# Lora A loaded in place by 32 register-addressed transfers instead of a gather and transposes

## What is computed

```python
# conditional layer, per sequence b
A, Bm = lora_As[itok], lora_Bs[itok]            # (32, 512, 16), (32, 16, 512)
xt = x @ W.T + b + 2 * ((x @ A) @ Bm)
# router
scores = softmax(xt @ router_w + router_b) + router_bias
gate = top 2 of the experts in the best 2 of 4 groups, weighted by their scores
# experts and shared expert
y = sum_e gate_e * ((silu(xt @ w1_e + b1_e) * (xt @ w2_e + b2_e)) @ w3_e + b3_e)
z = (silu(xt @ sw1 + sb1) * (xt @ sw2 + sb2)) @ sw3 + sb3
out = x + y + z
```

## Time and profile before

| | us |
|---|---|
| median of 3 runs (130.16 to 131.28) | 130.21 |
| the profiled execution's own time | 131.28 |
| its span, first to last instruction | 129.5 |
| PE busy in the span | 123.5 |
| DVE busy | 86.0 |
| ACT busy | 48.3 |

### The profile page before, as it was taken

One profiled execution on the slowest core, in us unless ns is written; L12 is line 12 of the kernel. 1 busy time (PEld: TensorE's weight loads), 2 busy tenths in 40 slices (PEclk: granted clock), 3 DMA queues, 4 the chain that ended last, 5 costly groups with the idle time before them and its releaser, 6 DMA issues.

```text
span 129.5 us, 2241 instructions
## 1 busy us (share of the span) xinstructions
PE 123.5 (95%) x815; PEld 102.3 (79%) x815; DVE 86.0 (66%) x194; ACT 48.3 (37%) x85; POOL 19.8 (15%) x33
## 2 busy tenths in 40 slices
PE   6999996999996999999999999999999999999991
PEld 6988874987885777888888889987788888888891
DVE  1496095497469718989999984355906279997731
ACT  1780373595559516203963574441022110000000
POOL 7374025000000020000027200033620000000000
PEclk9999999999999999999999999999999999999999
DMA  4999888659999699989305899402426999422222
GB/s 102 375 287 347 259 331 273 225 199 370 317 301 309 140 178 175 321 305 358 123 0 116 321 309 384 161 11 83 162 86 209 328 369 375 179 97 109 110 94 81
DMA packets 16908, 28.77 MB, mean 222 GB/s; under 512 B 1952, under 2 KB 6432, under 8 KB 16768
## 3 DMA queue, kind: packets, MB, share of 16 engines
q1 hardware_dynamic: 11728, 17.07, 40.5%
q10 hardware_dynamic: 3952, 7.34, 16.5%
q0 software_dynamic: 1216, 4.20, 10.3%
HBM read 19.17 MB, written 9.44 MB: 221 GB/s over the span
## 4 chain that ended last, share of the span: by engine, by line
PE 77%; DMA 9%; DVE 5%; ACT 3%; issue 2%; SPq 2%; DVEq 0%; ACTq 0%
PE bank L993 58%; DMA xT_raw<-in_xT 9%; PE bank L1192 6%; PE bank L1206 3%; PE bank L1049 2%; ACT xT_h L462 2%; PE bank L1267 1%; PE bank L1060 1%; PE bank L1037 1%; PE bank L1182 1%; SPq L319 1%; DVE sw_l L682 1%; ACT loraA_sb L472 1%; PE bank L1023 1%; PE bank L1097 1%
## 5 line engine op out<-in xcount | busy, mean ns | idle before, releaser
L993 PE MATMUL bank<-xtT_h,sw_h 128*128 128x512 f32 x32 | 12.9, 405 | 1.2 <-DVE sw_l L682 1.2
L993 PE MATMUL bank<-xtT_h,w12e_h 128*128 128x512 f32 x32 | 13.1, 409 | 0.0
L993 PE MATMUL bank<-xtT_h,w12e_l 128*128 128x512 f32 x32 | 12.5, 391 | 0.0
L993 PE MATMUL bank<-xtT_l,w12e_h 128*128 128x512 f32 x32 | 12.5, 391 | 0.0
L993 PE MATMUL bank<-xtT_h,sw_l 128*128 128x512 f32 x32 | 12.5, 390 | 0.0
L993 PE MATMUL bank<-xtT_l,sw_h 128*128 128x512 f32 x32 | 12.5, 390 | 0.0
L966 DVE SCALAR_TENSOR_TENSOR x_sb<-rows_sb,val,x_sb 128x512 f32<-128x512 f32 x16 | 11.7, 748 | 0.2
L972 DVE TENSOR_TENSOR x_sb<-x_sb,bank 128x512 f32<-128x512 f32 (+1 forms) x9 | 5.6, 626 | 4.8 <-PE bank L993 4.8
L682 DVE TENSOR_TENSOR xT_l<-xT_raw,xT_h 128x512 fp32r<-128x512 f32 (+1 forms) x6 | 5.2, 867 | 4.5 <-ACT xT_h L462 4.5
L993 PEld LDWEIGHTS bank<-xtT_h,sw_h 128*128 128x128 f32 x32 | 6.0, 188 | 2.8 <-DVE sw_l L682 1.4
L790 DVE SCALAR_TENSOR_TENSOR heT_sb<-bank,b_dense,sg_sb 128x512 f32<-128x512 f32 x4 | 3.0, 751 | 7.7 <-PE bank L993 7.7
(11 more groups left out here) (184 smaller groups left out, 294.1 us busy)
## 6 DMA issues: line engine op xcount, KB each, us to landing
y_rows<-zeros ACTq DMA_DIRECT2D x2, 2048.0 KB, 12.2
rows_sb<-y_rows SPq DMA_DIRECT2D x8, 512.0 KB, 8.4
xT_raw<-in_xT SPq DMA_DIRECT2D x8, 256.0 KB, 5.8
xt_rows<-xt_turned SPq DMA_DIRECT2D x8, 256.0 KB, 8.1
x_sb<-in_x SPq DMA_DIRECT2D x1, 2048.0 KB, 11.2
w_ring<-in_w_turned SPq DMA_DIRECT2D x4, 512.0 KB, 9.0
out<-x_sb ACTq DMA_DIRECT2D x7, 256.0 KB, 2.0
condW_raw<-in_condWT ACTq DMA_DIRECT2D x4, 256.0 KB, 4.5
```

Of the source, the lines that this page charges most:

```text
L993: mm = pe.matmul(out, a[p], b[q], start=(start and n == 0), stop=(stop and n == 2))
```

## The change

- A is laid out in memory as adapter, partition, rank, chunk. SP loads the A of each of the 32 sequences by a transfer of its own (128 partitions of 256 bytes), straight to the place from which PE reads it. The adapter's number is read from SBUF into a register of SP before each of them (`load_loraA`). The list of numbers (`seqs`) is loaded just before.
- `turn_lora` and `copy_loraA` go. POOL gathers only B, all four groups into buffers of their own, with nothing between them to wait for. The row numbers for that are made by DVE later, after the second chunk's rests.
- SP's order: the 32 loads are spread in four groups of eight, with the second half of x after the first group, the shared weights and three router tables after the second, and the other tables after the fourth.
- PE's order changes as shown below; the banks are renumbered, since bank 6 is free.
- DVE casts the first chunk of x; the rests of B and of the shared weights stay on DVE, but in other places; `turn_xt` of the first half moves behind the router's choice.

```diff
+            def load_loraA(g):
+                for s in range(g * SEQ_PER_GROUP, (g + 1) * SEQ_PER_GROUP):
+                    slot = sp.value_load(seqs_sb[0:1, s:s + 1], min_val=0, max_val=SLOTS - 1)
+                    sp.dma_start(loraA_sb[:, s * RANK:(s + 1) * RANK, :], lora_A[bass.ds(slot, 1)].rearrange("s p r k -> p (s r) k")
+                                 ).then_inc(loraA_in[g], 16)
             load_xT(0, 0)
-            sp.dma_start(slot_i[:], seq_slot).then_inc(seq_in, 16)
+            sp.dma_start(seqs_sb[:], seqs).then_inc(seqs_in, 16)
             for k in range(1, KC):
                 load_xT(0, k)
...
+            sp.dma_start(slot_i[:], seq_slot).then_inc(seq_in, 16)
+            sp.wait_ge(seqs_in, 16)
+            load_loraA(0)
+            for k in range(KC):
+                load_xT(1, k)
+            load_loraA(1)
+            sp.dma_start(sw12_raw[:], sw12).then_inc(sw12_in, 16)
+            sp.dma_start(condb_sb[:], cond_b).then_inc(router_in, 16)
+            sp.dma_start(rw_sb[:], router_w).then_inc(router_in, 16)
+            sp.dma_start(rb_col[:], router_b).then_inc(router_in, 16)
+            load_loraA(2)
+            load_loraA(3)
             sp.dma_start(rbias_sb[:], router_bias.partition_broadcast(P)).then_inc(small_in, 16)
             sp.dma_start(sb12_sb[:], sb12).then_inc(small_in, 16)
             sp.dma_start(b12_sb[:], b12).then_inc(small_in, 16)
-            sp.wait_ge(xT_in[KC - 1], 16)
-            for k in range(KC):
-                load_xT(1, k)
-            sp.wait_ge(lora_in[1], 16)
-            sp.dma_start(sw12_raw[:], sw12).then_inc(sw12_in, 16)
...
 # POOL
+            pool.memset(zeros[:], 0.0).then_inc(zeros_set, 1)
+            pool.wait_ge(lora_row_ready, 1)
+            for g in range(GROUPS_L):
+                pool.indirect_dma_start(lora_raw[:, g, :], None, lora_B,
                                         bass.IndirectOffsetOnAxis(ap=lora_row[:, g:g + 1], axis=0)).then_inc(lora_in[g], 16)
...
 # ACT
             for k in range(KC):
                 hi_condW(k)
-                hi_xT(0, k, k + 1)
+                if k >= 1:
+                    hi_xT(0, k, k + 1)
+            hi_loraB(0)
             hi_xT(1, 0, 2)
-            hi_loraB(0)
-            copy_loraA(0)
             hi_xT(1, 2, 4)
             hi_loraB(1)
             hi_lhT(0)
-            copy_loraA(1)
+            hi_sw12(0)
             hi_lhT(1)
...
 # DVE
+            dve.wait_ge(xT_in[0], 16)
+            dve.tensor_copy(xT_split[0][0][:, 0, :], xT_raw[0][:, 0, :]).then_inc(first_hi, 1)
...
             mask_lh(0)
+            lo_sw12(0)
             mask_lh(1)
             for m in range(KC):
-                turn_xt(0, m)
                 lo_xtT(0, m)
             lo_lora(2)
-            lo_sw12(0)
+            lo_lora(3)
+            lo_sw12(1)
             mask_lh(2)
-            lo_lora(3)
-            dve.wait_ge(small_in, 16 * 6)
+            mask_lh(3)
+            dve.wait_ge(small_in, 16 * 3)
             shift_logits(0)
-            mask_lh(3)
+            turn_xt(0, 0)
             choose(0)
-            lo_sw12(1)
+            for m in range(1, KC):
+                turn_xt(0, m)
...
 # PE
             def lora_h(g):
...
-                pe.wait_ge(loraA_copied, g + 1)
+                pe.wait_ge(loraA_in[g], 16 * SEQ_PER_GROUP)
...
-            cond_first(0)
-            cond_first(1)
-            cond_first(2)
-            pe.wait_ge(consts_ready, 4)
-            turn_lora(0)
-            cond_first(3)
+            for k in range(KC):
+                cond_first(k)
             lora_h(0)
-            turn_lora(1)
-            cond_second(0, 0, KC // 2)
+            cond_second(0, 0, KC)
             lora_h(1)
-            cond_second(0, KC // 2, KC)
+            cond_second(1, 0, KC)
             cond_lora(0)
-            cond_second(1, 0, KC)
-            turn_lora(2)
             cond_second(2, 0, KC)
             lora_h(2)
             logits_turned(0)
-            turn_lora(3)
+            lora_h(3)
             cond_second(3, 0, KC // 2)
+            pe.wait_ge(consts_ready, 4)
             logits(0)
-            lora_h(3)
             cond_second(3, KC // 2, KC)
             cond_lora(1)
```

More of the change, by code:

```diff
@@ L102, in program @@
         w12e_raw = at(8, "w12e_raw", [P, DENSE, W12])
-        zeros = at(16, "zeros", [P, DIM])
+        loraA_sb = at(16, "loraA_sb", [P, SEQS * RANK, KC])
+        zeros = at(148, "zeros", [P, DIM])
         w3e_raw = at(16, "w3e_raw", [P, DENSE, DIM])
@@ L221, in program @@
         w3_in = [sem(f"w3_in{s}") for s in range(STATIC)]
+        loraA_in = [sem(f"loraA_in{g}") for g in range(GROUPS_L)]
         lora_in = [sem(f"lora_in{g}") for g in range(GROUPS_L)]
@@ L268, in cond_bank @@
         def cond_bank(n, m):
-            return bank[(4, 0, 1, 2)[m] if n else m]
+            return bank[(4, 6, 0, 1)[m] if n else m]
         def unit_of(u):
@@ L285, in gate_bank @@
         def gate_bank(s):
-            return bank[(4, 0)[s % 2]]
+            return bank[(4, 6)[s % 2]]
         def up_bank(s):
@@ L518, in _ @@
             hi_lhT(0)
-            copy_loraA(1)
+            hi_sw12(0)
             hi_lhT(1)
-            act.wait_ge(small_in, 16 * 6)
-            for m in range(KC):
+            act.wait_ge(router_in, 16 * 3)
+            for m in range(2):
                 whole_xtT(0, m)
                 hi_xtT(0, m)
+            for m in range(2, KC):
+                whole_xtT(0, m)
+            for m in range(2, KC):
+                hi_xtT(0, m)
+            hi_loraB(2)
+            hi_loraB(3)
             act.wait_ge(zeros_set, 1)
-            act.wait_ge(lora_in[3], 16)
             for k in range(K):
@@ L610, in _ @@
                 act.wait_ge(gateT_done, n + 1)
-                act.copy(gateT[:, n * 512:(n + 1) * 512], bank[(5, 6)[n]][0:STACK, :]).then_inc(gateT_copied, 1)
+                act.copy(gateT[:, n * 512:(n + 1) * 512], bank[(5, 2)[n]][0:STACK, :]).then_inc(gateT_copied, 1)
             act.wait_ge(w3e_in, 16 * DENSE)
@@ L689, in lo_xT @@
                 hi, lo = xT_split[n]
-                dve.wait_ge(xT_hi, last if n == 0 else KC + last // 2)
+                if n == 0 and first == 0:
+                    dve.wait_ge(first_hi, 1)
+                else:
+                    dve.wait_ge(xT_hi, first if n == 0 else KC - 1 + last // 2)
                 rest(lo[:, first:last], xT_raw[n][:, first:last], hi[:, first:last], xT_done)
@@ L707, in mask_lh @@
                 dve.wait_ge(lhT_hi, g + 1)
-                rest(lhT_split[1][:, g % 2], lhT_sb[:], lhT_split[0][:, g % 2], lhT_done)
+                rest(lhT_split[1][:, g], lhT_sb[:], lhT_split[0][:, g], lhT_done)
             def lo_xtT(n, m):
@@ L754, in _ @@
                 lo_xT(0, k, k + 1)
+                if k == 1:
+                    dve.wait_ge(seq_in, 16)
+                    then(dve.tensor_copy(slot_f[:], slot_i[:]))
+                    then(dve.tensor_scalar(slot_f2[:], slot_f[:], float(RANK), None, ALU.mult))
+                    dve.tensor_scalar(lora_row[:], slot_f2[:], part16[:, 0:1], None, ALU.add).then_inc(lora_row_ready, 1)
             then(dve.tensor_copy(cols[:], cols_i[:, 0:BPAD]))
@@ L1012, in cond_second @@
             def cond_second(m, first, last):
-                if m >= 1 and first == 0:
-                    pe.wait_ge(xtT_hi, m)
+                if m >= 2 and first == 0:
+                    pe.wait_ge(xtT_hi, m - 1)
                 for k in range(first, last):
@@ L1049, in cond_lora @@
                             mm = pe.matmul(cond_bank(n, m)[:, at:at + GT], loraB_split[q][:, g % 2, m * P:(m + 1) * P],
-                                           lhT_split[p][:, g % 2, :], start=False, stop=(p == 1 and g % 2 == 1))
+                                           lhT_split[p][:, g, :], start=False, stop=(p == 1 and g % 2 == 1))
                     mm.then_inc(cond_done, 1)
@@ L1166, in _ @@
             for i in range(TILES):
-                mm = pe.transpose(bank[(5, 6)[i // 4]][0:STACK, (i % 4) * P:(i % 4 + 1) * P], gate[:, i, :], ident[:])
+                mm = pe.transpose(bank[(5, 2)[i // 4]][0:STACK, (i % 4) * P:(i % 4 + 1) * P], gate[:, i, :], ident[:])
                 if i % 4 == 3:
```

91 lines of the change are left out of this document (31 added, 60 removed).

## The result

| | before | after |
|---|---|---|
| median, us (4 runs each) | 130.62 | 154.19 |
| lowest to highest | 130.16 to 131.28 | 153.53 to 155.34 |
| span of the profiled execution | 129.5 | 153.6 |
| PE busy in it | 123.5 | 127.2 |
| mean granted clock of PE | 0.998 | 0.933 |

The ratio is 1.181, with a 95% interval of 1.171 to 1.191. Forecast were 144.3 us and a range up to 150.5: the direction is right, the size is not.

A forecast was written before the change was run, and what follows sets the result against it. PE, busy 84.89 of 84.91 us from 42.04, was the bound, with SP's serial loads deciding its delay. 11.7 + 2.4 = 14.1 us on a 129.5 us span gave 143.6, median 144.3 us; range 139.0 to 150.5.

The forecast's parts named there:

- 32 steps of 1.09 are 34.88: On SP, each number read plus its issue takes 1.09 us; 32 in series put the last load of A at 42.77.
- the landing: A's last 32 KB load takes 4.2 us from issue to arrival, bounds 3.4 and 7.8, allowing for the zeros written meanwhile.
- The rival of a dearer step: On SP, each read and issue takes 1.29 us instead of 1.09, adding 6.4 us: 150.7 us; chance 0.10.
- The clock was a rival: PE's clock falls while it stands ahead of `lora_h(3)`, and later products lose up to 2.3 us: 146.6 us; chance 0.18.
- the 53.8 forecast: Start of the shared expert on PE: A in at 47.0 plus 6.79 us of work, instead of 42.04, so +11.7 us.
- The hole was to be 4.4 us: PE reaches `lora_h(3)` at 42.6 and waits 4.4 us there for A's fourth group, in at 47.0.
- The dense weights: Behind the shared expert, late turns delay stores, `x_sb` and then `w12e`, so PE waits: +0.6 to +5, taken as +2.4 us.
- the 14.1 us forecast: Total slowdown of the span: 11.7 us ahead of the shared expert plus 2.4 us behind it.
- What was costed at nothing: Earlier PE waits lie under the wait for A; first cast on DVE, B-only gather, banks, buffers and earlier zeros add 0.
- The best case of 3.9 us: Most the change could gain on PE before the shared expert: holes of 1.07 and 1.19 us plus four transposes at 0.41.
- The weights of A at a stride: In `lora_h(3)`, weights read at a stride of four numbers might double its 0.65 us; taken as 0.
- the 155 us: On SP, a `tensor_load` floor of about 600 ns would add 10.6 us over 32 reads, some 155 us; rejected for the trace.

The follow-up runs named there:

- both big terms gone: The changed kernel with adapter numbers written in as constants, so SP reads none, and the first half's turns back ahead of the router's choice: 131.59 us, ratio 1.006.
- three moved lines: The kernel before, with ACT's copy of A's second group earlier and the shared weights' second cast and rest right behind the first: 128.94 us, ratio 0.986.

## Why the prediction was wrong in size

- **Where it is decided: right.** It named SP's 32 steps, `lora_h(3)` as the place and 1.09 us as the step. The first eight loads keep it, and with fixed addresses 17.5 us go.
- **The step that failed: "32 steps of 1.09 are 34.88".** In the changed kernel they take 40.2 (8.97, 9.36 and 21.87), and the last issue, which was to start at 42.77, starts at 48.07, 5.3 us later. Six reads at 0.90 to 0.98 make 5.67 - 6 x 0.27 = 4.05 of it; most of the rest are single delays in the second eight (8.62 instead of 8.00) and ahead of the last issue. The text itself put the zeros into this stretch and charged them to the landing, which was in fact shorter (3.15 from issue to product, not 4.2); the read, of which it had four rows beside other transfers, was taken as fixed. The rival of a dearer step had a size of 6.4 but the wrong reason, and a chance of 0.10.
- **The clock was a rival and is a term.** From `lora_h(3)` to the shared expert 8.42 us instead of 6.79: +1.6, where the rival's price was up to 2.3. The sum 5.3 - 1.05 + 1.63 is the 5.9 us by which the shared expert starts later than the 53.8 forecast. The hole was to be 4.4 us by the forecast and became 10.9; the clock fell in the smaller hole of 4.0 ahead of the dense weights too.
- **The dense weights: the mechanism right, the size too small.** Stores from 61.41, `x_sb` behind them, `w12e` behind `x_sb`: a wait of 4.0 and not 2.4. Counted from a shared expert 5.9 us later, the first store (forecast 55.4) and PE's arrival (78.3, measured 84.31) are where they were to be; the eight stores take 8.61 us to issue and not 6.8, and `x_sb` 12.5 to land and not 11.2. Some 2.2 us of half clock come behind it (5.68 us for fifteen products, of which 15 x 0.23 = 3.4 are wanted at the full clock), a term that the sum did not have. (The first of the four turns stands ahead of the choice, not behind it; the stores wait for all four.) Together these are 6.2 of the 6.5 us behind the shared expert.
- **The rivals were not alternatives.** A dearer step, the clock and a longer wait for the dense weights each had a price and a chance of its own, and the range was drawn as if one of them at a time could come true. One cause, A being late, makes the hole in which the clock falls; all three came together: the 14.1 us forecast, 5.9 more ahead of the shared expert, and 6.5 - 2.4 = 4.1 more behind it make the 24.1 measured.
- **What was costed at nothing.** The waits for x (4.0), for the second group (0.4) and for the second mask (3.3) lay under the wait for A, as said: PE stood in front of `lora_h(3)` at 51.22 - 10.87 = 40.35, forecast 42.6. The best case of 3.9 us was too good: with both big terms gone, moving `lora_h(3)` forward makes a wait of 2.6 us by itself. The weights of A at a stride, taken as free, cost little: 32 instructions of `lora_h` take 0.72 us at the full clock instead of 0.65.

The floor of about 600 ns that the Trainium skill ("DMA: Bandwidth & Descriptors", Latency and other measured facts) gives for a `tensor_load` is not borne out where the reads are undisturbed, 0.26 to 0.28 us; 0.90 to 0.98 beside the zeros lie above it. That the 155 us which the prediction worked out by it lie close to the measured 154.2 is luck: 25 of the 32 reads took 0.26 to 0.28 us, and the time beyond the forecast came from the six reads beside the zeros, the clock and the dense weights. That idleness brings the throttled clock back, as "TensorE: Matmul & The Clock Gate" of the Trainium skill says (Part 1: The HAM clock gate), this trace now shows: 0.50 granted from 45.33 to 55.57, after PE had stood still from 40.35 on. The prediction found no row for it in the trace before, but one was there, behind PE's last product, with PE at rest and a mean clock of 0.90:

```profile
126.95:129.50 2.55, 0.00 (x0) 0.00 (x0) 0.42 (x1) 0.00 (x0) 0.00 (x0) 0.90 0.22 74
```

## What to carry to other kernels

A register read and the issue that uses it are a serial step on their queue, here 1.09 us for a transfer of 32 KB, and 1.7 to 1.8 beside the zeros; count the steps, add what else stands in that queue, and compare the last landing with the moment of use before replacing one gather by many addressed loads. Where one late transfer opens a hole, the half clock behind the hole and the transfers queued behind it belong to the same case: add them instead of weighing them against each other. Holes of an engine can be closed by order alone: three moved lines gave 1.4% here, where the whole change cost 18%.

## What the runs showed of the hardware

- SP's read of a number out of SBUF takes 0.27 us, 0.46 the first time, and 0.86 to 0.98 while 4 MB of zeros go from SBUF to memory (375 GB/s in all from 37 to 48 us). It stayed at 0.27 beside a copy of as many bytes within device memory (384 GB/s), and while the 1 MB of shared weights came in, near 25 to 30 us.
- An issue with an address in a register takes no longer than one with a fixed address: 0.33 us when reads stand between, against 0.43 (median) for fixed addresses in a row, which make a step of 0.46.
- PE's granted clock went to half in or just behind holes of 10.9, 6.1 and 4.0 us, of 2.4 us in the run with late zeros (0.50 from 34.09 to 37.50), and once, with forty products in the hole, behind 1.7 us of rest. It stayed at 1.00 with 1.6 us of rest in another run, and through a hole of 3.3 us in the changed kernel (29.84 to 33.31). So the length of a hole alone does not tell whether the clock falls.
